# Attention row maxima: scores through PSUM one bank at a time instead of in pairs of banks

## The reference

```
q  = (ql @ Wqu) per head (16 heads of 16),  qr = rope((ql @ Wqr) per head, 64)
k  = (ckv @ Wku) per head,                  kr = rope(x @ Wkr, 64), shared by the heads
scores = (q.k + qr.kr) / sqrt(80), causal mask, softmax over the keys
out    = (softmax(scores) @ v) @ Wo
```

## Time and profile before

| | |
|---|---|
| median of 3 runs | 3030.85 us (3026.89 to 3036.65) |
| the profiled execution | 3017.37 us, its span 3015.5 us |
| mean granted TensorE clock | 0.945 of full speed |
| PE busy over the span | 2595.8 us (86%) |
| DVE busy over the span | 1750.5 us (58%) |
| ACT busy over the span | 1474.8 us (49%) |
| the attention stage | from about 295 to 1190 us |
| line 1245 (the maxima) | 384 instructions, 332.1 us busy |
| line 1106 (their matmuls) | 640 matmuls |

### The profile page before, as it was taken

The page is one execution under the profiler, slowest core; times in us unless marked ns, Lnnn a source line. Parts: engine busy times, 40 slices in busy tenths (PEclk is TensorE's granted clock), DMA queues, the critical chain, the costliest instruction groups (busy, mean ns, idle before and its releaser), DMA issues. The chain is left out here.

```text
span 3015.5 us, 41808 instructions
## 1 busy us (share of the span) xinstructions
PE 2595.8 (86%) x14798; PEld 1985.8 (66%) x14798; DVE 1750.5 (58%) x3106; ACT 1474.8 (49%) x2916; POOL 1044.4 (35%) x943
## 2 busy tenths in 40 slices
PE   4976889899889898596998989888968998888898
PEld 4765555555555554585887767667757887777687
DVE  6456764764764771655445898988853334334353
ACT  2435546546547545243225976777754334333232
POOL 1552211211211210264231433333344567666332
PEclk9988999999999999598998999989989999999999
DMA  4232000000000000324000000000032223233200
GB/s 142 78 121 70 15 8 22 17 8 22 17 8 15 17 1 9 117 83 143 28 13 31 0 1 8 1 8 1 8 106 68 74 84 97 85 91 87 75 31 28
DMA packets 70264, 138.62 MB, mean 46 GB/s; under 512 B 16817, under 2 KB 38025, under 8 KB 68913
## 3 DMA queue, kind: packets, MB, share of 16 engines
q0 software_dynamic: 26336, 73.01, 8.2%
q1 hardware_dynamic: 43728, 62.95, 6.4%
HBM read 114.71 MB, written 20.81 MB: 45 GB/s over the span
## 5 line engine op out<-in xcount | busy, mean ns | idle before, releaser
L1379 ACT ACTIVATE PT<-ps 128x512 f32<-128x512 f32 (+3 forms) x640 | 313.3, 534 | 318.0 <-PE ps L1130 175.6
L2172 POOL DMA_INDIRECT KV<-kv_scratch,sidx x384 | 367.5, 957 | 239.6 <-issue 126.8
L1245 DVE TENSOR_REDUCE xn<-ps 128x1 f32<-128x1024 f32 (+7 forms) x384 | 332.1, 907 | 110.4 <-PE ps L1106 84.0
L35 PE MATMUL ps<-KIh,qih 128*128 128x512 f32 (+2 forms) x640 | 251.3, 393 | 63.5 <-DVE Isc L1800 38.2
L36 PE MATMUL ps<-KIl,qih 128*128 128x512 f32 (+2 forms) x640 | 242.3, 379 | 0.0
L37 PE MATMUL ps<-KIh,qil 128*128 128x512 f32 (+2 forms) x640 | 242.0, 378 | 0.0
L1800 DVE SCALAR_TENSOR_TENSOR Isc<-ps,iw,Isc 128x1024 f32<-128x1024 f32 (+7 forms) x216 | 208.8, 967 | 53.4 <-ACT ps L1713 47.4
L1127 PE MATMUL ps<-qB,KB 128*128 128x512 f32 (+2 forms) x640 | 235.2, 367 | 0.0
L1713 ACT ACTIVATE ps<-ps,iwa 128x1024 f32<-128x1024 f32 (+7 forms) x240 | 198.0, 857 | 62.6 <-PE ps L37 62.2
L1412 POOL TENSOR_TENSOR rr<-rb 128x512 f32<-128x512 f32 x64 | 82.2, 1284 | 347.8 <-DVE rb L1235 344.5
L1415 POOL TENSOR_TENSOR qB<-rr,qA 64x512 fp32r<-64x512 f32 x64 | 81.5, 1274 | 344.8 <-ACT qB L1369 344.6
(11 more groups left out here) (347 smaller groups left out, 7024.6 us busy)
## 6 DMA issues: line engine op xcount, KB each, us to landing
cs<-in_rope SPq DMA_DIRECT2D x20, 512.0 KB, 4.2
w1raw<-in_w SPq DMA_DIRECT2D x16, 512.0 KB, 4.2
ycomb<-y_rows SPq DMA_DIRECT2D x16, 512.0 KB, 5.0
KV<-kv_scratch,sidx POOLq DMA_INDIRECT x384, 2.8
w2raw<-in_w SPq DMA_DIRECT2D x16, 256.0 KB, 5.2
xn_rows<-xnr SPq DMA_DIRECT2D x8, 512.0 KB, 4.0
whr<-in_whead SPq DMA_DIRECT2D x16, 256.0 KB, 2.8
wir<-in_wi SPq DMA_DIRECT2D x1, 2176.0 KB, 8.0
```

The costliest lines, as they stand in the source:

```text
L35: pe.matmul(out, lhs[0], rhs[0], start=start, stop=False)
L1245: v.tensor_reduce(mp[:, CT * h + r, k:k + 1], o[:, 0:end], AX_X, ALU.max).then_inc(a_free, 1)
L1379: s.activation(PT[:, rnd % 2, hh, lo:CH], ps[:, ST_BANKS[e % 3], lo:CH], ACT.Exp, scale=SCALE).then_inc(a_exp, 1)
L2172: g.indirect_dma_start(KV[:, BG * (k % RB) + m, :], None, a["kv_scratch"], bass.IndirectOffsetOnAxis(sidx[:, t % 2, at:at + 1], 0)).then_i ...
```

## The change

Every piece of step M becomes one bank wide. The step has c + 1 pieces in place of c // 2 + 1; no bank is left out any more. TensorE waits for each bank's room before its matmul and signals each bank when it is written; VectorE takes one maximum for each bank (up to 512 elements) into its own column of `mp`, and releases it; the last maximum over the columns (step X) reads c + 1 of them.

```diff
@@ bank ring
-            for k_ in range({"K": 2, "P": 3, "M": u_ % NCH // 2 + 1, "R": 1, "F": 1, "G": 2}.get(kind_, 0)):
+            for k_ in range({"K": 2, "P": 3, "M": u_ % NCH + 1, "R": 1, "F": 1, "G": 2}.get(kind_, 0)):
                 key_ = kind_, u_, h_, r_, k_
-                wide_ = 2 if kind_ == "M" and 2 * k_ + 1 <= u_ % NCH else 1
-                if at_bank + wide_ > RING or (wide_ == 2 and at_bank % 2):
-                    at_bank = (at_bank + 1) % RING
                 PIECE[key_], BANK[key_] = pieces, at_bank
-                ROOM[key_] = max(user[at_bank:at_bank + wide_])
+                ROOM[key_] = user[at_bank]
                 pieces += 1
-                for b_ in range(at_bank, at_bank + wide_):
-                    user[b_] = pieces
-                at_bank = (at_bank + wide_) % RING
+                user[at_bank] = pieces
+                at_bank = (at_bank + 1) % RING
@@ TensorE, step M
                     for s in range(c + 1):
-                        if s % 2 == 0:
-                            pe.wait_ge(a_free, ROOM[kind, u, h, r, s // 2])
-                        o = ps[:, BANK[kind, u, h, r, s // 2] + s % 2, :]
+                        pe.wait_ge(a_free, ROOM[kind, u, h, r, s])
+                        o = ps[:, BANK[kind, u, h, r, s], :]
...
-                        if s % 2 == 1 or s == c:
-                            i.then_inc(a_full, 1)
+                        i.then_inc(a_full, 1)
@@ VectorE, steps M and X
-                    for k in range(c // 2 + 1):
-                        v.wait_ge(a_full, PIECE[kind, u, h, r, k] + 1)
-                        b = BANK[kind, u, h, r, k]
-                        end = min(2 * CH, (CT * c + r + 1) * P - 2 * CH * k)
-                        o = ps[:, b:b + 2, :].rearrange("p b s -> p (b s)") if end > CH else ps[:, b, :]
+                    for k in range(c + 1):
+                        o = full(kind, u, h, r, k)
+                        end = min(CH, (CT * c + r + 1) * P - CH * k)
                         v.tensor_reduce(mp[:, CT * h + r, k:k + 1], o[:, 0:end], AX_X, ALU.max).then_inc(a_free, 1)
                 elif kind == "X":
-                    v.wait_ge(a_free, PIECE["M", u, GH - 1, CT - 1, c // 2] + 1)
+                    v.wait_ge(a_free, PIECE["M", u, GH - 1, CT - 1, c] + 1)
...
-                    v.tensor_reduce(mcol[:], mp[:, :, 0:c // 2 + 1], AX_X, ALU.max).then_inc(a_mc, 1)
+                    v.tensor_reduce(mcol[:], mp[:, :, 0:c + 1], AX_X, ALU.max).then_inc(a_mc, 1)
```

## The result

The changed kernel takes 2977.76 us (median of 4 runs, 2975.69 to 2981.69) where the kernel before takes 3028.87 (4 runs, 3023.61 to 3036.65): ratio 0.983, 95% interval 0.981 to 0.986. The profiled execution took 2981.7 us, span 2979.8.

The account below looks back on a forecast made before the run. TensorE was taken to bound the attention, with small idle pieces waiting for VectorE's maxima. Terms 14 + 3 + 3 + 1.6 - 1.5 gave 20 us faster, from 3030.85 to 3011 us; range 2993 to 3028.

Parts of the forecast that it names:

- c = 2: Attention phases preparing queries of chunk 2, one per four-head group: shorter TensorE waits for maxima, 3.5 us each, 14 in all.
- the clock: TensorE's granted clock in c = 2 phases: shorter idle pieces remove some dips, 3 us gained, bounds 0 and 5.
- c = 3: Phases of chunk 3: M steps even, what comes behind them gains 0.8 us a phase, 3 in all.
- c = 1: Phases of chunk 1: F and the first M behind a P gain 0.4 us a phase, 1.6 in all.
- the bursts' tails: End of c = 1 bursts: VectorE some 0.3 us later, delaying the chain to `mrow`; -1 to -3, taken as -1.5 us.
- the price of a split: VectorE, each pair's maximum made two: 140 ns taken per split, 256 splits, 36 us more VectorE work.
- half of each long wait: c = 2 bursts: a TensorE wait of the 1.22 us kind keeps half; 1.1 us gained of 2.44 in one burst.
- F behind an M step: c = 3: F's 0.77 us wait for a pair shortens, since single bank 0 would be free at 870.56, not 871.39.
- The 256 more met waits and increments: TensorE's added semaphore operations: bounds 0 and, at 0.02 us each, +5 us; taken as 0.
- (c): Rival: c = 2 waits vanish whole (29), clock dips (5), F's and first M's (5): -39, 2992 us; chance 0.13.
- (a): Rival: VectorE becomes the pace, c = 1 and c = 3 bursts pay every split: +10, 3041 us; chance 0.08.
- The rule of the Trainium skill on the count of operations: VectorE: minimize chained operations, not semaphores; taken as the whole answer, 36 us lost, the far end of (a).

Follow-up runs that it names:

- the kernel with the 16-element maximum: Changed kernel plus an unused VectorE maximum over 16 elements of the same bank before every second maximum, 256 in all: ratio 0.989 to the kernel before.
- the kernel with the 256-element maximum: Changed kernel plus an unused VectorE maximum over 256 elements of the same bank before every second maximum: ratio 1.003 to the kernel before.
- the old banks: Changed kernel with a bank again left out where a pair would have had to start at an even bank, single releases kept: ratio 0.987 to before.
- one bank less: Changed kernel with a ring of three banks in place of four: ratio 1.005 to the kernel before, c = 2 phase 49.93 us.

## Why the prediction was wrong

The place, the direction and the mechanism stood; the terms were too small, by 22 of the 42 us that the traced stage gained. By the terms of the sum: c = 2 gave 24 us at equal clock where 14 were reckoned, the clock 5 where 3, c = 3 7.6 where 3, c = 1 5.9 where 1.6, and the bursts' tails took nothing where 1.5 were taken off.

**The failed step: the price of a split, 138 to 147 ns** ("2 x 679 - 1220"). It took recorded durations for occupancy. Maxima in a row overlap in the record. These are rows of the timeline of the kernel after, read in narrow windows, so that each begins with another maximum; the count at the end is how many the row holds:

```profile
800.74 1.29 DVE L1237 TENSOR_REDUCE xn<-ps 128x1 f32<-128x512 f32 x2 [2.06 <-PE ps L1101]
...
801.35 1.48 DVE L1237 TENSOR_REDUCE xn<-ps 128x1 f32<-128x512 f32 x3
...
802.14 1.28 DVE L1237 TENSOR_REDUCE xn<-ps 128x1 f32<-128x512 f32 x2
802.74 1.01 DVE L1237 TENSOR_REDUCE xn<-ps 128x1 f32<-128x512 f32 x2
803.34 1.01 DVE L1237 TENSOR_REDUCE xn<-ps 128x1 f32<-128x256 f32 x2
```

From 800.74 to 801.35, and from 802.14 to 802.74 to 803.34, is 0.60 to 0.61 us for a maximum whose record says 0.68; over all 386 in unbroken rows of this trace the median is 0.60. In the kernel before, a 1024-element one takes 1.14 from start to start, the median of 128 as well:

```profile
891.98 2.09 DVE L1245 TENSOR_REDUCE xn<-ps 128x1 f32<-128x1024 f32 x2 [0.16 <-PE ps L1106]
893.12 2.19 DVE L1245 TENSOR_REDUCE xn<-ps 128x1 f32<-128x768 f32 x2
894.08 2.22 DVE L1245 TENSOR_REDUCE xn<-ps 128x1 f32<-128x1024 f32 x2
```

2 x 0.60 - 1.14 = 0.06 us. It stood in the rows of the prediction itself: the earlier trace rows give 2.36 us for two maxima of 1.22 each. With the right price the 36 us become 15, and the kernel before with its maxima split shows just that, 15.8. The changed kernel's VectorE has only 8.1 more, because its rows of maxima are less broken: 99 maxima stand before a pause in place of 163, and only there does the whole recorded duration count as busy. At 0.08 us each that is some 5 of the 7.7 us between the two.

What this did to the sum is shown by the kernel with the 16-element maximum, in which a split costs what I thought: its c = 3 phases gain 0.8 us, the forecast, against 1.9 measured, and its c = 1 phases some 0.6 against 0.4 forecast, with 1.3 to 1.6 measured. At c = 3 the gain also lies where it was forecast: F stands 1.0 us nearer to the start of the phase, and between F and the last M step nothing is gained or lost to within 0.2 us. So nearly all that was missed at c = 3 and c = 1 is this price, and some 11 us in all.

**The second: how far the waits at c = 2 go.** I kept half of each long wait and reckoned 3.5 us a phase; 6.0 is measured at equal clock (53.7 to 47.7), and with my own price of a split, in the kernel with the 16-element maximum, it is still 5.3. The starts of the four M steps of one burst, before and then after, both at a clock of 1.00:

```profile
1050.27 0.83 PE L1106 MATMUL ps<-XTl,qA 128*128 128x512 f32 x3
1052.39 0.82 PE L1106 MATMUL ps<-XTl,qA 128*128 128x512 f32 x3 [1.22 <-DVE xn L1245]
1054.51 0.88 PE L1106 MATMUL ps<-XTl,qA 128*128 128x512 f32 x3 [1.22 <-DVE xn L1245]
1056.62 0.94 PE L1106 MATMUL ps<-XTl,qA 128*128 128x512 f32 x3 [0.21 <-DVE xn L1245]
```

```profile
1013.28 0.83 PE L1101 MATMUL ps<-XTl,qA 128*128 128x512 f32 x3
1013.98 1.54 PE L1101 MATMUL ps<-XTl,qA 128*128 128x512 f32 x3
1015.43 1.55 PE L1101 MATMUL ps<-XTl,qA 128*128 128x512 f32 x3
1017.80 0.94 PE L1101 MATMUL ps<-XTl,qA 128*128 128x512 f32 x3
```

First to last 6.35 us became 4.52: 1.83 gained where 1.1 was reckoned; the others gave 1.2, 1.5 and 1.9 (0.65, 0.7 and 1.0 reckoned). The reckoning of the burst was sound as far as it went, and it stopped at the third M step. It had that step out at about 4.0 us; its last matmul ends at 3.93 us after the burst's start in the kernel with the 16-element maximum and at 3.77 in the changed one, where it was 5.19. The fourth ends at 5.70 and 5.54, where it was 7.37, so it adds 0.4 us that had no place in the sum. Before, every M step of this burst stands 2.11 or 2.12 us behind the last, as do four of the six in the two earlier bursts of the phase, where the recorded wait is often only 0.2 with S scores between. For those I had counted the recorded wait as the most that could go. But a matmul is recorded at 0.39 us while the next can start 0.23 after it, and a mask matmul at 0.23 where the next can follow after 0.04 (the shortest distances in the trace of before). In the earlier trace rows the idle 1.22 us before 828.83 begins with the recorded end of a mask matmul that started at 827.38; the next matmul could have started some 0.19 earlier than that end, so the wait was 1.41. Each of the 71 waits of the earlier trace rows is understated in this way, and one shorter than that has no row. This is worked out from rows; no run tested it alone. Once an M step needs no pair, the second one of the burst follows the first at 0.70 us, without a pause.

**The clock.** I took 3 of at most 5 us. The traces bear out the upper bound: five of the eight c = 2 phases of the two traces of before ran at 0.94 to 0.97, against one of eight in the two traces of after. It seems to do more in the timed runs of the kernel before, none of which has a trace here: nine of them ran at mean granted clocks of 0.937 to 0.943 (median 3027.0 us), while the two traced executions have 0.945 and 0.944, in 3017.4 and 3019.6 us; the changed kernel has 0.944 or 0.945 throughout. That may be why the medians differ by 47 to 51 us and the traced executions by 36 to 38, but it is not shown, and it stays open. So does a loss of 4 to 7 us in the later stages of the traced executions (from the last reciprocal to the end of the span 1824.6 and 1827.5 us before, 1831.4 and 1831.8 after). The matmuls there are the same 9316; PE's busy time is 5.9 us more in the first pair of traces and 0.8 in the second, and the granted clock 0.93 before and 0.92 after.

**The rest.** c = 3 and c = 1 gained 1.9 and about 1.5 us a phase, outside the 1 us of the prediction, for the price above. F behind an M step goes as worked out: its wait of the earlier trace rows is gone, and it follows the M step's first matmul at 1.17 us (837.86 to 839.03) where it followed at 1.94 (869.45 to 871.39). The tails of the bursts cost nothing seen (I took -1.5). The 256 more met waits and increments cost nothing seen: an M step at 401.56 has its four matmuls in 0.97 us as in the earlier trace rows. The 0.02 us each that I gave as their bound came from no row, and no run shows it.

```profile
837.86 1.10 PE L1101 MATMUL ps<-XTh,qA 128*128 128x512 f32 x4
838.29 2.48 DVE L1237 TENSOR_REDUCE xn<-ps 128x1 f32<-128x512 f32 x4 [0.48 <-PE ps L1101]
...
839.03 1.13 PE L1140 MATMUL ps<-xn,spread 128*128 128x512 f32 x2
```

Of the rivals, (c), in which more goes than reckoned, was the nearest, and the result passed it by 14 us. (a) needs a price of a split near 0.4 us, as the kernel with the 256-element maximum shows (0.06 + 0.33). The rule of the Trainium skill on the count of operations ("VectorE: DVE Perf Modes", "Rules for kernel authors") holds in sign, +0.19% for the split alone, at less than half the size that I gave it. The trace agrees with that of the Trainium skill's "Perfetto Trace Analysis", "Matmuls", on groups rotating through the banks: waits of 42.7 us became 6.1, though the left-out bank by itself is worth only 1.0 of the 6.0 us at c = 2 once the releases are single.

## What to carry to other kernels

Price an added instruction by the distance from start to start in a row of its kind, not by recorded durations: here 0.06 us, not 0.14. Read waits on TensorE the same way, since by the spacings above the record understates them by about 0.2 us apiece. When producer and consumer idle in turn at a fixed period (2.12 us here), look at the unit of hand-over: halving it gave 5.0 of the 6.0 us with the old banks, and 3.8 with one bank less. (More banks for the pairs were not tried; all eight are in use.) Follow a burst to its last step before adding it up. And ask what a dearer instruction would cost before fearing it; by the estimate above this split could have cost five times as much.

## What the runs showed of the hardware

- Maxima over 512 PSUM elements in a row start 0.60 us apart, over 1024 1.14, over 256 0.33, with recorded durations of 0.68, 1.22 and 0.41.
- A VectorE memset of one element per partition, recorded at 59 ns, cost some 0.01 us in such a row; a 16-element maximum over PSUM, recorded at 162 ns, cost 0.08.
- Phases of c = 2 with pairs of waits of 1.22 us in a burst ran at a mean granted clock of 0.94 to 0.97 in five of eight cases and at 1.00 in three, 2.1 us apart (0.94 against 1.00). In the two traces of the changed kernel, without those waits, seven of eight ran at 1.00. The waits are not the only thing that goes with a dip: the first phase of c = 2 ran at 0.93 in the kernel with the old banks and at 0.97 in the one with the 16-element maximum.
